# Score products over the 48 rows that hold parts, without zero fills, in a decoder layer with two attentions and experts

## The chip, the cores and the metric

The kernel runs on one core of one Trainium2 chip. The metric is the device time of one execution, in microseconds (us), as the median of the timed runs. One execution was taken by the profiler.

## What is computed

Input are x and a context, 16 batches of 128 tokens by 128 features in fp32. Both attentions have 16 heads of 8 features. Cut to what matters:

```
q, k, v = heads(x @ Wq.T + bq), heads(x @ Wk.T + bk), heads(x @ Wv.T + bv)
eq, ek  = heads(x @ Weq.T + beq), heads(x @ Wek.T + bek)
scores  = q k^T * SCALE
esc     = eq ek^T * SCALE * decay          # decay = exp(-0.1 |i - j|)
attn    = softmax(scores + 0.5 * esc)
ctx     = attn @ mixed(v)                  # v plus two gated, head-wise products
x = layernorm(x + layernorm(x + ctx @ Wo.T + bo) * ln_g + ln_b)
x = layernorm(x + cross_attention(x, context, context))   # plain softmax attention
x = layernorm(x + experts(x))              # 16 experts, top 4, silu(g) * u, all computed densely
```

## The kernel before

**Parts.** The score products are made in bf16 with the accuracy of fp32: each projected q and k is split into three bf16 parts (high, middle, lowest), and six products of parts are summed by one matmul. So a head's contraction has 6 parts x 8 features = 48 rows (`NP = 6`, `HD = 8`, `R = NP * HD`). The parts are written to DRAM (`spill`) and read back in the order of rows (`stack1`, `stack2`) into the buffers `stk[0]` and `stk[1]`: partitions 0 to 47 hold the parts, for q and k, all heads and, in the first attention, both kinds (plain and entangled). Partitions 48 to 127 are filled with zeros once at the start, and every score matmul contracts over all 128 partitions:

```
dst = stk[b.par][:].rearrange("p a h u t -> p a h (u t)")
sp.dma_start(dst[0:R, :, at:at + H // 2], src[:, :, at:at + H // 2]
```

`stk2` is the same memory, cut in four for the second attention. Later the expert layer uses `stk` as scratch.

**Stages.** Set-up (weights transposed, first parts), first attention, second attention, expert layer. In the attentions every engine runs a program written out by hand: a slot is one step over the batches, a unit (0 to 3 in a slot) is a group of four heads, and each operation works on the batch of its own lag. Engines are tied by semaphores alone, and each works strictly in its program's order. Loops over slots are hardware loops with the same body.

**TensorE in the first attention, unit by unit** (line numbers as in the profile; four matmuls each unless said):
- every unit: entangled scores L699 (`entangled_score`); then what the unit has of its own; scores L709 (`score`); then the rest of its own; then the maximum of the unit before is subtracted by a matmul, L717 (one, 512 columns), and the probabilities of two units before are transposed, L727.
- of its own: unit 0 the output product L816 between L699 and L709; unit 1 the weighted sum L789 (16 matmuls over 32 columns of weights) between them and the transposes L803 at the end; unit 2 projections L677 between them and behind L709; unit 3 L789 between them and L812 behind L709.

VectorE multiplies the entangled scores by the decay (L1463), adds and takes the maximum (L1475); ScalarE takes the exponent (L1143) and copies the transposed probabilities (L1169) and the sums `pvs` (L1178).

**TensorE in the second attention:** every unit: L738 (`score2`, scores into bank 0, of which VectorE's L1486 takes the maximum; the next L738 waits for it), L760 (`score_t`, the same scores transposed), L767 (the maxima are subtracted, four matmuls). Behind that: unit 1 L789 and L812; unit 2 L816 and then L751 (one transpose of the maxima, 16 columns of weights); unit 3 L789 and L803. Unit 0 begins with the projections L687 and L688. ScalarE's exponent is L1153.

**Zero fills.** VectorE's first instruction fills `stk[0]` (L1384), GpSimd fills `stk[1]` behind its loads of biases (L469), VectorE fills `top_t` (L1386). SyncE waits for the first two before the first `stack1` of each buffer.

Of the kernel before, what the change touches and what calls it, by code (L numbers as in the profile page):

```python
# [13 lines left out]
F32 = mybir.dt.float32  # L14
# [26 lines left out]
R = NP * HD  # L41
# [42 lines left out]
def head(g, j):  # L84

    return 2 * GH * (g // 2) + 2 * j + g % 2
# [8 lines left out]
def build(nc, a, k, out):  # L95
    with ExitStack() as ctx:  # L96
        def sb(name, shape, dt=F32):
            return ctx.enter_context(nc.sbuf_tensor(name, shape, dt))

        def sem(name):  # L100
            return ctx.enter_context(nc.semaphore(name))
# [52 lines left out]
        stk = [sb(f"stk{p}", [128, 2, H, 2, S], BF16) for p in range(2)]  # L154

        stk2 = [stk[k % 2][:].rearrange("p a h u t -> p a (h u t)")[:, :, k // 2 * H * S:k // 2 * H * S + H * S]
                .rearrange("p a (h t) -> p a h t", t=S) for k in range(4)]
# [12 lines left out]
        top_t = sb("top_t", [128, 2, S], BF16)  # L170
# [41 lines left out]
        bank = [ctx.enter_context(nc.psum_tensor(f"bank{i}", [128, 512], F32)) for i in range(8)]  # L212
# [58 lines left out]
                self.var_eps = sem(f"var_eps{n}")  # L271
                self.rstd = sem(f"rstd{n}")
        L1, L2 = Layer(1, slice(0, 2)), Layer(2, slice(0, 1))
        zeroed = [sem("zeroed0"), sem("zeroed1"), sem("zeroed2")]
        TAIL1, TAIL2 = 3, 5
        root = [sem("root0"), sem("root1")]
        root_step = [sem("root_step0"), sem("root_step1")]
# [42 lines left out]
        E_BANK = (2, 5)  # L320
# [4 lines left out]
        def _(sp):  # L325
# [23 lines left out]
            def spill(L, b):  # L349

                sp.wait_ge(L.low, b.n + 1)
                if L is L1:
                    src = by_part[b.par].rearrange("p k u t -> p k (u t)")
                    dst = scr1[bass.ds(b.n, 1)].rearrange("b a s p u t -> p (b a) s (u t)")
                else:
                    src = by_part[b.par][:, :, 0, :]
                    dst = scr2[bass.ds(b.n, 1)].rearrange("b a s p t -> p (b a) s t")
                for side in range(2):
                    sp.dma_start(dst[:, side, 0:3], src[:, 3 * side:3 * side + 3]).then_inc(L.spilled[b.par], 16)
                    sp.dma_start(dst[:, side, 3:5], src[:, 4 * side:4 * side + 2]).then_inc(L.spilled[b.par], 16)  # L360
                sp.dma_start(dst[:, :, 5], src[:, HIGH]).then_inc(L.spilled[b.par], 16)

            def stack1(b, half):

                if half == 0:
                    sp.wait_ge(L1.spilled[b.par], b.pair * L1.spill_step + L1.spill_step)
                if not isinstance(b.n, int) or b.n >= 2:
                    sp.wait_ge(L1.scores, NG * b.n - NG - NM + NM * half)
                src = scr1[bass.ds(b.n, 1)].rearrange("b a s (f h) u t -> (b s f) a h (u t)", h=H)
                dst = stk[b.par][:].rearrange("p a h u t -> p a h (u t)")  # L370
                at = H // 2 * half
                sp.dma_start(dst[0:R, :, at:at + H // 2], src[:, :, at:at + H // 2]
                             ).then_inc(L1.stacked[2 * b.par + half], 16)
# [12 lines left out]
            def pair1(p):  # L386
                for par in range(2):
                    b = Batch(p, par)
                    if isinstance(p, int) and p == 0:
                        sp.wait_ge(zeroed[par], 1)  # L390
                    stack1(b, 0)
                    if b.back(-1).live:
                        spill(L1, b.back(-1))
                    stack1(b, 1)

            spill(L1, Batch(0, 0))
            pair1(0)
            load_ffn()
            with sp.Fori(1, NB // 2 - 1) as p:
                pair1(p)  # L400
            pair1(NB // 2 - 1)

            def quad2(q):
# [47 lines left out]
        def _(pool):  # L451
            def rows(dst, src):
                n = src.shape[0]
                pool.dma_start(dst, src.unsqueeze(0).broadcast_to([128, n])).then_inc(in_rows, 16)
# [11 lines left out]
            rows(ln_b[:], a["L0_attn_ln_b"])  # L466
            rows(bv2[:], a["L0_xattn_bv"])
            rows(bo2[:], a["L0_xattn_bo"])
            pool.memset(stk[1][:].rearrange("p a h u t -> p (a h u t)").bitcast(F32), 0.0).then_inc(zeroed[1], 1)  # L469
            pool.memset(minus_half[:], -0.5)  # L470
            pool.memset(eps_col[:], EPS)
            pool.memset(zero_col[:], 0.0)
# [194 lines left out]
        def _(pe):  # L667
# [23 lines left out]
            def entangled_score(b, g):  # L691

                u = b.n * NG + g
                if g in (0, 2):
                    pe.wait_ge(L1.stacked[2 * b.par + g // 2], b.pair * 16 + 16)
                if not isinstance(u, int) or u >= 2:
                    pe.wait_ge(L1.picked, u - 1)
                for j in range(GH):
                    m = pe.matmul(bank[E_BANK[g % 2]][:, 128 * j:128 * j + 128], stk[b.par][:, 0, head(g, j), 1, :],  # L699
                                  stk[b.par][:, 1, head(g, j), 1, :], start=True, stop=True)  # L700
                m.then_inc(L1.ent_scores, 1)

            def score(b, g):

                u = b.n * NG + g
                if not isinstance(u, int) or u >= 2:
                    pe.wait_ge(L1.exped, u - 1)
                for j in range(GH):
                    m = pe.matmul(bank[g % 2][:, 128 * j:128 * j + 128], stk[b.par][:, 0, head(g, j), 0, :],  # L709
                                  stk[b.par][:, 1, head(g, j), 0, :], start=(j == 0), stop=True,  # L710
                                  skip_group_check=True)
                m.then_inc(L1.scores, 1)

# [16 lines left out]
            def score2(b, g):  # L730

                u = b.n * NG + g
                if g == 0:
                    pe.wait_ge(L2.stacked[b.buf], b.quad * L2.stack_step + L2.stack_step)
                if not isinstance(u, int) or u >= 1:
                    pe.wait_ge(L2.maxed, u)
                for j in range(GH):
                    m = pe.matmul(bank[0][:, 128 * j:128 * j + 128], stk2[b.buf][:, 0, head(g, j), :],  # L738
                                  stk2[b.buf][:, 1, head(g, j), :], start=True, stop=True)
                m.then_inc(L2.scores, 1)  # L740

            def turn_top(b):
# [11 lines left out]
            def score_t(b, g):  # L754

                u = b.n * NG + g
                if not isinstance(u, int) or u >= 2:
                    pe.wait_ge(L2.exped, u - 1)
                for j in range(GH):
                    pe.matmul(bank[2 + g % 2][:, 128 * j:128 * j + 128], stk2[b.buf][:, 1, head(g, j), :],  # L760
                              stk2[b.buf][:, 0, head(g, j), :], start=(j == 0), stop=True,
                              skip_group_check=True)
                if g == 0:
                    pe.wait_ge(L2.top_t_ev, b.n + 1)
                for j in range(GH):
                    h = GH * g + j
                    m = pe.matmul(bank[2 + g % 2][:, 128 * j:128 * j + 128],  # L767
                                  neg_ident[:, h:h + 1].broadcast_to([128, 128]), top_t[:, b.par, :],
                                  start=False, stop=True, skip_group_check=True)
                m.then_inc(L2.shifted, 1)  # L770
# [108 lines left out]
            for i, w in enumerate((WQ, WEQ, WK, WEK)):  # L879
                t = pe.transpose(bank[0][:, 128 * i:128 * i + 128], wn[:, w, :], ident[:])  # L880
# [20 lines left out]
            for i, w in enumerate((WV, WO, XQ, XK)):  # L901
                t = pe.transpose(bank[1][:, 128 * i:128 * i + 128], wn[:, w, :], ident[:])
# [20 lines left out]
            for b in range(NB):  # L923
                if b >= 4:
                    pe.wait_ge(dve_set, DV_WALL + b - 3)
                pe.matmul(bank[b % 4][:, 0:VSZ], x_t[:, 128 * b:128 * b + 128], wall[:],
                          start=True, stop=True).then_inc(pe_set, 1)
# [4 lines left out]
            for c in range(4):  # L932
                pe.wait_ge(act_set, c + 2)
                for j in range(4):
                    t = pe.transpose(bank[C_BANK[c]][:, 128 * j:128 * j + 128], c_tok[:, 4 * c + j, :], ident[:])
# [165 lines left out]
        def _(act):  # L1101
# [54 lines left out]
            def take_top(b):  # L1156
                act.wait_ge(L2.top_t, b.n + 1)
                if isinstance(b.n, int) and b.n == 0:
                    act.wait_ge(zeroed[2], 1)
                if not isinstance(b.n, int) or b.n >= 2:  # L1160
                    act.wait_ge(L2.shifted, NG * b.n - NG)
                act.copy(top_t[0:H, b.par, :], bank[6][0:H, 256:256 + S // 2].bitcast(BF16)).then_inc(L2.top_t_ev, 1)
# [206 lines left out]
        def _(dve):  # L1369
            made = [0]  # L1370

            def step(ins):
                made[0] += 1
                ins.then_inc(dve_set, 1)
                return made[0]
# [5 lines left out]

                dve.memset(waiter[:, n:n + 1], 0.0)

            dve.memset(stk[0][:].rearrange("p a h u t -> p (a h u t)").bitcast(F32), 0.0).then_inc(zeroed[0], 1)  # L1384
            step(dve.memset(half_pi[:], math.pi / 2))
            dve.memset(top_t[:].rearrange("p a t -> p (a t)").bitcast(F32), 0.0).then_inc(zeroed[2], 1)  # L1386

            dve.wait_ge(in_bias, 7 * 16)
            n = step(dve.tensor_copy(bias_perm[:].rearrange("r (f h) -> r f h", h=H),
# [412 lines left out]
```

## Time and profile before

| | us |
|---|---|
| timed runs, median (lowest to highest) | 391.68 (390.48 to 393.94) |
| the profiled execution | 396.48 |
| its span, first to last instruction | 394.7 |
| busy: TensorE matmuls | 341.8 (87%) |
| busy: TensorE weight loads | 263.2 (67%) |
| busy: VectorE | 271.2 (69%) |
| busy: ScalarE | 224.1 (57%) |
| busy: GpSimd | 217.6 (55%) |
| mean granted TensorE clock | 0.959 of full |

The engines are called PE (TensorE's matmuls), PEld (its weight loads), DVE (VectorE), ACT (ScalarE), POOL (GpSimd) and SP (SyncE) in the rows. The ends of matmuls are modelled, so their busy times overlap; starts are what was recorded. "128*32" is the shape of the stationary operand, rows by columns. Idle time is given with what ended it: "issue" means that nothing which the profile shows held the instruction up.

### The profile page before, as it was taken

The page shows a single profiled execution, that of the slowest core. Times are in us where ns is not written, and L with a number is a line of the kernel's source. Part 1 is how long each engine was busy: PE and PEld are TensorE (multiplying, and loading weights), DVE is VectorE, ACT ScalarE, POOL GpSimd, SP SyncE. Part 2 cuts the span into 40 slices and gives each one's busy share as a digit, 9 for nine tenths or more (in the row PEclk, how much of TensorE's full clock was granted, in tenths as well). Part 3 has the DMA queues.
Part 4 walks back from the last instruction along what each step waited for, and adds up shares of the span by engine and source line. Part 5 has one row for each costly group of instructions (what it writes and reads, how often), then busy time and mean ns, then how long its engine had stood idle before and what let it go on. Part 6 is the DMA issues. An engine that isn't in the chain of part 4 may idle for free. (4 is left out here: it accounts for less than half of the span.)

```text
span 394.7 us, 11535 instructions
## 1 busy us (share of the span) xinstructions
PE 341.8 (87%) x3556; PEld 263.2 (67%) x3556; DVE 271.2 (69%) x1247; ACT 224.1 (57%) x527; POOL 217.6 (55%) x405
## 2 busy tenths in 40 slices
PE   2885899999999997986789899998796999999992
PEld 1764778777887776774678777777563756566662
DVE  5643999999999997965446667666953149644453
ACT  1546487899989985685566667664461341222220
POOL 8777345788888984885743333320114244655551
PEclk9989599999999999998799999999999899999997
DMA  6989898789899887246344655671006420443410
GB/s 120 233 226 202 164 219 199 163 208 201 201 181 197 190 189 171 54 91 150 84 98 111 149 131 141 129 149 28 2 22 195 139 75 7 96 151 102 139 28 27
DMA packets 76927, 52.89 MB, mean 134 GB/s; under 512 B 34448, under 2 KB 68064, under 8 KB 76880
## 3 DMA queue, kind: packets, MB, share of 16 engines
q1 hardware_dynamic: 75840, 51.73, 56.0%
q0 software_dynamic: 512, 0.48, 0.9%
q8 instruction: 24, 0.39, 0.5%
q14 instruction: 23, 0.19, 0.2%
q10 hardware_dynamic: 528, 0.10, 0.2%
HBM read 32.24 MB, written 20.05 MB: 132 GB/s over the span
## 5 line engine op out<-in xcount | busy, mean ns | idle before, releaser
L1475 DVE CUSTOM_DVE_ANT_0 bank<-bank,decayed_e 128x128 f32<-128x128 f32 x256 | 67.2, 325 | 1.1 <-issue 0.5
L1486 DVE TENSOR_REDUCE top<-bank 128x4 bf16<-128x512 f32 x64 | 44.2, 690 | 29.5 <-PE bank L738 29.1
L646 POOL TENSOR_TENSOR stk<-stk 128x512 f32<-128x512 f32 x32 | 40.7, 1276 | 40.8 <-ACT stk L1349 39.3
L1153 ACT ACTIVATE prob_t<-bank 128x512 f32<-128x512 f32 x64 | 38.1, 597 | 34.0 <-PE bank L767 33.5
L1721 DVE TENSOR_TENSOR stk<-bank,stk 128x512 f32<-128x512 f32 x32 | 22.1, 692 | 46.1 <-POOL stk L646 45.0
L1349 ACT ACTIVATE stk<-bank 128x512 f32<-128x512 f32 x32 | 19.0, 597 | 54.5 <-PE bank L1049 53.0
L481 POOL TENSOR_TENSOR rest<-pf,parts 128x512 f32<-128x512 f32 (+1 forms) x32 | 29.2, 914 | 37.3 <-ACT parts L1132 37.1
L1143 ACT ACTIVATE prob<-bank 128x512 f32<-128x512 f32 x64 | 39.3, 613 | 17.4 <-PE bank L717 16.8
L789 PE MATMUL bank<-prob_t,vmix 128*32 128x128 f32 x1024 | 43.0, 281 | 5.9 <-ACT pvs L1178 5.9
L487 POOL TENSOR_TENSOR parts<-rest,parts 128x512 bf16<-128x512 f32 (+1 forms) x32 | 29.2, 914 | 30.1 <-ACT parts L1136 30.0
L1062 PEld LDWEIGHTS bank<-w,stk 128*128 128x128 f32 x256 | 33.4, 193 | 17.1 <-issue 8.6
L1463 DVE TENSOR_TENSOR decayed_e<-bank,decay 128x512 f32<-128x512 f32 x64 | 44.0, 688 | 0.3 <-issue 0.3
L727 PE MATMUL bank<-ident,prob 128*128 128x128 f32 x256 | 39.8, 279 | 0.0
L1169 ACT COPY prob_t<-bank 128x512 f32<-128x512 f32 x64 | 38.4, 600 | 1.0 <-PE bank L727 1.0
L1475 DVE DVE_READ_ACCUMULATOR2_ANT shift<- 128x1 bf16 x256 | 37.1, 145 | 0.0
L738 PE MATMUL bank<-stk 128*128 128x128 bf16 x256 | 26.2, 227 | 12.0 <-DVE top L1486 10.8
L727 PEld LDWEIGHTS bank<-ident,prob 128*128 128x128 f32 x256 | 31.0, 143 | 6.7 <-issue 2.5
L1062 PE MATMUL bank<-w,stk 128*128 128x128 f32 x256 | 34.3, 278 | 0.9 <-DVE stk L1721 0.9
L789 PEld LDWEIGHTS bank<-prob_t,vmix 128*32 128x32 f32 x1024 | 26.0, 110 | 13.2 <-issue 7.9
L1053 PE MATMUL bank<-x_t,w 128*128 128x512 f32 x64 | 33.6, 607 | 0.0
L1049 PE MATMUL bank<-x_t,w 128*128 128x512 f32 x64 | 33.5, 606 | 0.0
L738 PEld LDWEIGHTS bank<-stk 128*128 128x128 bf16 x256 | 17.7, 103 | 18.5 <-DVE top L1486 11.4
(201 smaller groups left out, 804.8 us busy)
## 6 DMA issues: line engine op xcount, KB each, us to landing
stk<-parts_dram SPq DMA_DIRECT2D x32, 384.0 KB, 5.5
stk<-shares_dram SPq DMA_DIRECT2D x64, 128.0 KB, 3.0
parts_dram<-parts SPq DMA_DIRECT2D x32, 192.0 KB, 2.4
parts_dram<-parts SPq DMA_DIRECT2D x48, 128.0 KB, 2.4
stk<-parts_dram SPq DMA_DIRECT2D x32, 192.0 KB, 3.7
parts_dram<-parts SPq DMA_DIRECT2D x32, 96.0 KB, 2.0
parts_dram<-parts SPq DMA_DIRECT2D x48, 64.0 KB, 1.8
w<-in_L_ffn_w_dram SPq DMA_DIRECT2D x3, 512.0 KB, 9.2
```

The lines of the kernel that those rows point to most:

```text
L646: pool.tensor_tensor(h1[kk % 2], sg[kk % 2], share[kk], ALU.mult).then_inc(weighted, 1)
L727: t = pe.transpose(bank[3][:, 128 * j:128 * j + 128], prob[g % 2][:, j, :], ident[:])
L738: m = pe.matmul(bank[0][:, 128 * j:128 * j + 128], stk2[b.buf][:, 0, head(g, j), :], stk2[b.buf][:, 1, head(g, j), :], start=True, stop=True)
L789: w = pe.matmul(bank[at][32 * j:32 * j + 32, 128 * m:128 * m + 128], vmix[b.par][:, head(2 * m, j) // 2, e:e + 2, :].rearrange("p e f -> p ...
L1053: pe.matmul(bank[UP_BANK[u % 3]][:], w3[:, 128 * kk:128 * kk + 128], xt, start=True, stop=True).then_inc(up_mm, 1)
L1062: m = pe.matmul(bank[4 + c % 2][:, 128 * t:128 * t + 128], actt[u % 3][:, 128 * t:128 * t + 128], w2[:, kk, :], start=(kk == 0 and t == 0) ...
L1143: act.activation(prob[g % 2][:].rearrange("p h t -> p (h t)"), bank[g % 2][:], ACT.Exp).then_inc(L.exped, 1)
L1153: act.activation(prob_t[g][:].rearrange("p h t -> p (h t)"), bank[2 + g % 2][:], ACT.Exp).then_inc(L2.exped, 1)
L1169: act.copy(prob_t[g][:].rearrange("p h t -> p (h t)"), bank[3][:]).then_inc(L.turned_ev, 1)
L1463: dve.tensor_tensor(decayed_e[:, g % 2], bank[E_BANK[g % 2]][:].rearrange("p (h t) -> p h t", h=GH), decay[:].unsqueeze(1).broadcast_to([1 ...
L1475: m = dve.tensor_tensor_reduce(out=bank[g % 2][:, 128 * j:128 * j + 128], in0=bank[g % 2][:, 128 * j:128 * j + 128], in1=decayed_e[:, g % ...
L1486: dve.tensor_reduce(top[:, b.par, GH * g:GH * g + GH], bank[0][:].rearrange("p (h t) -> p h t", h=GH), AX.X, ALU.max).then_inc(L2.maxed, 1)
```

## The change

All score matmuls of both attentions (L699, L709, L738, L760) take partitions 0 to 47 of both operands instead of all 128. The two fills of `stk` go, and with them SyncE's waits. The fill of `top_t` stays. No other instruction is added, removed or moved on any engine.

```diff
-        zeroed = [sem("zeroed0"), sem("zeroed1"), sem("zeroed2")]
+        zeroed = sem("zeroed")
...
-                    if isinstance(p, int) and p == 0:
-                        sp.wait_ge(zeroed[par], 1)
                     stack1(b, 0)
...
-            pool.memset(stk[1][:].rearrange("p a h u t -> p (a h u t)").bitcast(F32), 0.0).then_inc(zeroed[1], 1)
...
-                    m = pe.matmul(bank[E_BANK[g % 2]][:, 128 * j:128 * j + 128], stk[b.par][:, 0, head(g, j), 1, :],
-                                  stk[b.par][:, 1, head(g, j), 1, :], start=True, stop=True)
+                    m = pe.matmul(bank[E_BANK[g % 2]][:, 128 * j:128 * j + 128], stk[b.par][0:R, 0, head(g, j), 1, :],
+                                  stk[b.par][0:R, 1, head(g, j), 1, :], start=True, stop=True)
...
-                    m = pe.matmul(bank[g % 2][:, 128 * j:128 * j + 128], stk[b.par][:, 0, head(g, j), 0, :],
-                                  stk[b.par][:, 1, head(g, j), 0, :], start=(j == 0), stop=True,
+                    m = pe.matmul(bank[g % 2][:, 128 * j:128 * j + 128], stk[b.par][0:R, 0, head(g, j), 0, :],
+                                  stk[b.par][0:R, 1, head(g, j), 0, :], start=(j == 0), stop=True,
                                   skip_group_check=True)
...
-                    m = pe.matmul(bank[0][:, 128 * j:128 * j + 128], stk2[b.buf][:, 0, head(g, j), :],
-                                  stk2[b.buf][:, 1, head(g, j), :], start=True, stop=True)
+                    m = pe.matmul(bank[0][:, 128 * j:128 * j + 128], stk2[b.buf][0:R, 0, head(g, j), :],
+                                  stk2[b.buf][0:R, 1, head(g, j), :], start=True, stop=True)
...
-                    pe.matmul(bank[2 + g % 2][:, 128 * j:128 * j + 128], stk2[b.buf][:, 1, head(g, j), :],
-                              stk2[b.buf][:, 0, head(g, j), :], start=(j == 0), stop=True,
+                    pe.matmul(bank[2 + g % 2][:, 128 * j:128 * j + 128], stk2[b.buf][0:R, 1, head(g, j), :],
+                              stk2[b.buf][0:R, 0, head(g, j), :], start=(j == 0), stop=True,
                               skip_group_check=True)
...
-            dve.memset(stk[0][:].rearrange("p a h u t -> p (a h u t)").bitcast(F32), 0.0).then_inc(zeroed[0], 1)
             step(dve.memset(half_pi[:], math.pi / 2))
```

## Rows read from the trace of the kernel before

**Rows 1.** Busy time by stretch: us, PE, PEld, DVE, ACT, POOL, clock, DMA, GB/s.

```profile
37.90:175.30 137.40, 125.63 (x1519) 105.09 (x1520) 126.92 (x833) 111.00 (x266) 100.73 (x237) 0.96 0.81 175
175.30:292.00 116.70, 102.17 (x1509) 82.39 (x1507) 75.38 (x234) 70.93 (x183) 42.34 (x95) 0.96 0.45 100
```

**Rows 2.** Timeline, PE, first attention: start, us, operation, idle before in brackets.

```profile
99.46 0.38 PE L803 MATMUL bank<-ident,pvs 128*128 128x128 f32 x2
...
101.34 0.60 PE L727 MATMUL bank<-ident,prob 128*128 128x128 f32 x4
101.77 0.39 PE L699 MATMUL bank<-stk 128*128 128x128 bf16 x4
102.09 0.67 PE L789 MATMUL bank<-prob_t,vmix 128*32 128x128 f32 x16
102.69 0.40 PE L709 MATMUL bank<-stk 128*128 128x128 bf16 x4
102.92 0.28 PE L812 MATMUL bank<-ident,attn_o 128*128 128x128 f32 x1
103.04 0.38 PE L717 MATMUL bank<-shift,neg_ident 128*128 128x512 bf16 x1
...
103.69 0.39 PE L699 MATMUL bank<-stk 128*128 128x128 bf16 x4
103.91 0.44 PE L816 MATMUL bank<-wo_t,attn_ot 128*128 128x128 f32 x2
104.26 0.40 PE L709 MATMUL bank<-stk 128*128 128x128 bf16 x4
...
105.29 0.39 PE L699 MATMUL bank<-stk 128*128 128x128 bf16 x4
106.13 0.67 PE L789 MATMUL bank<-prob_t,vmix 128*32 128x128 f32 x16 [0.46 <-ACT pvs L1178]
...
107.62 0.38 PE L803 MATMUL bank<-ident,pvs 128*128 128x128 f32 x2
```

**Rows 3.** Timeline, PEld, first attention, behind the weighted sum.

```profile
102.68 0.23 PEld L709 LDWEIGHTS bank<-stk 128*128 128x128 bf16 x4 [0.20 <-issue]
```

**Rows 4.** Timeline, PE and PEld, set-up: the transposes of the last weights.

```profile
12.73 0.64 PE L905 MATMUL bank<-ident,wn 128*128 128x128 f32 x2
13.30 0.34 PE L906 MATMUL bank<-ident,gates_n 48*128 48x48 f32 x1
...
12.95 0.42 PE L905 MATMUL bank<-ident,wn 128*128 128x128 f32 x1
...
13.30 0.18 PEld L906 LDWEIGHTS bank<-ident,gates_n 48*128 48x128 f32 x1 [0.33 <-issue]
```

**Rows 5.** Timeline, PE, second attention.

```profile
226.05 0.39 PE L738 MATMUL bank<-stk 128*128 128x128 bf16 x4
...
226.72 0.44 PE L816 MATMUL bank<-xw_t,attn_ot 128*128 128x128 f32 x2
227.09 0.22 PE L751 MATMUL bank<-ident_bf,top 128*16 128x128 bf16 x1
227.25 0.40 PE L738 MATMUL bank<-stk 128*128 128x128 bf16 x4
...
229.78 0.39 PE L767 MATMUL bank<-top_t,neg_ident 128*128 128x128 bf16 x4
230.51 0.40 PE L738 MATMUL bank<-stk 128*128 128x128 bf16 x4 [0.34 <-DVE top L1486]
```

**Rows 6.** A stretch at half clock: its busy times (columns as in rows 1), and PE's timeline.

```profile
195.20:197.50 2.30, 2.30 (x24) 1.69 (x22) 0.23 (x1) 0.89 (x2) 0.94 (x2) 0.50 0.03 5
...
195.49 1.10 PE L789 MATMUL bank<-prob_t,vmix 128*32 128x128 f32 x16
196.52 0.80 PE L687 MATMUL bank<-x_t,xw_t 128*128 128x128 f32 x2
```

**Rows 7.** Timeline of the set-up: DVE, POOL and PE around the second zero fill.

```profile
9.41 4.62 DVE L1412 TENSOR_SCALAR bv_cols<-bv_cols,bias_t 128x128 f32<-128x128 f32 x1
9.61 4.49 DVE L1414 TENSOR_SCALAR neg_ident<-ident 128x128 bf16<-128x128 f32 x1
...
9.75 3.53 POOL L469 MEMSET stk<- 128x4096 f32 x1
...
15.46 1.53 PE L889 MATMUL bank<-ident,x_tok 128*128 128x128 f32 x12 [0.26 <-DMA x_tok<-in_x_dram]
```

More of the change, by code:

```diff
@@ L1158, in take_top @@
                 if isinstance(b.n, int) and b.n == 0:
-                    act.wait_ge(zeroed[2], 1)
+                    act.wait_ge(zeroed, 1)
                 if not isinstance(b.n, int) or b.n >= 2:
@@ L1382, in carry @@
                 dve.memset(waiter[:, n:n + 1], 0.0)
-            dve.memset(stk[0][:].rearrange("p a h u t -> p (a h u t)").bitcast(F32), 0.0).then_inc(zeroed[0], 1)
             step(dve.memset(half_pi[:], math.pi / 2))
-            dve.memset(top_t[:].rearrange("p a t -> p (a t)").bitcast(F32), 0.0).then_inc(zeroed[2], 1)
+            dve.memset(top_t[:].rearrange("p a t -> p (a t)").bitcast(F32), 0.0).then_inc(zeroed, 1)
             dve.wait_ge(in_bias, 7 * 16)
```

## The prediction

> **What bounds the kernel now.** I read the busy times by stage first [rows 1]. They split the 394.7 us span into a set-up, the stretch of the first attention (37.9 to 175.3 us), that of the second (175.3 to 292.0 us) and the expert layer behind it. The diff edits two things: 1024 of TensorE's matmuls with their weight loads (four groups of 256: 16 batches by 16 heads), which all lie in the two middle stretches, and two zero fills in the set-up. In the first attention VectorE is busy for 126.92 of 137.40 us and TensorE for 125.63: both are nearly full, and neither has much to give. In the second VectorE has 75.38 of 116.70 and TensorE 102.17, so there TensorE sets the pace.
>
> Busy time does not say how much room TensorE has, since the ends of its matmuls are modelled and overlap. Starts do. So next I read TensorE's timeline over one slot (one batch) of the first attention [rows 2]. A slot lasts 107.62 - 99.46 = 8.16 us, from one L803 to the next. Four 128-column bf16 matmuls take 0.22 to 0.23 us from their start to the next group's start (102.69 to 102.92, 103.69 to 103.91), that is 0.055 us each. The only idle time printed in that slot is 0.46 us before the weighted sum L789 of unit 1. Measured by starts it is 106.13 - 105.29 = 0.84 us, where the same pair in unit 3 takes 102.09 - 101.77 = 0.32: 0.52 us of slack a slot. That is all the room TensorE has there.
>
> **Narrower contraction, the matmuls themselves.** A matmul streams its moving columns, 128 before and after, and the stationary operand keeps 128 columns. None of the spacings above contains the number of rows. Nearest row: L906 contracts over 48 rows, its load takes 0.18 us and its matmul 0.34 against 0.42 for the 128-row transposes L905 [rows 4]; but it also streams only 48 columns, 80 fewer, which at the 1.2 GHz level is 0.067 us of the 0.08. So the shape itself is worth between nothing and 0.02 us a matmul in latency, and nothing in spacing. I take nothing.
>
> **Narrower contraction, its neighbours.** This is the term that counts. Today all score matmuls have the shape of what stands around them, 128 rows by 128 columns, and the load of the next stationary operand is drawn ahead of the running matmuls. Where the shape changes, the trace shows that it isn't:
> - Into the weighted sum (128*32): the last of four bf16 matmuls starts at 101.77 + 0.165 = 101.94, and L789 at 102.09: 0.155 us where 0.055 is usual. A change costs 0.10 us [rows 2].
> - Out of it, TensorE's weight loads stand still for 0.20 us, and the releaser is "issue", so no semaphore holds them [rows 3].
> - Out of the 128*16 transpose L751 into the scores: 227.25 - 227.09 = 0.16 us, again 0.10 more than 0.055. Into it, behind fp32: the second L816 starts 0.165 us after 226.72, so L751 comes 0.20 us later, where fp32 neighbours follow each other in 0.11 (four L727 and the next group: 101.77 - 101.34 = 0.43). (The second L816 is 0.44 less one such matmul's 0.28 behind the first.) Again 0.09 to 0.10 [rows 2, 5].
> - Is a change of rows alone enough? One instruction tells: L906 stands behind two L905 with no wait between, loads 48*128 instead of 128*128, and its load stood idle for 0.33 us "issue". The second L905 starts at 12.95 and L906 at 13.30: 0.35 us, where the two L905 lie 0.22 apart [rows 4]. At the same matmul length (0.42, the level at which 195.49 stands) the exit from the 128*32 shape takes 196.52 - (195.49 + 1.10 - 0.42) = 0.35 us [rows 6]. The row change costs just what the column change costs there. This row decides my forecast.
>
> The Trainium skill, page "TensorEngine Tiling (Array Packing)", section "Key Properties", has a rule for this: changing the tiling mode drains TensorE, and its list of modes has row tiles of 64 for a contraction up to 64. The trace agrees, with its 0.35 us before L906 [rows 4]; the rule says nothing of the price. By the rule with that price the sum is the one below, by a chip without it the sum would be nothing.
>
> So I count shape changes by the order of the program, unit by unit. First attention, before: into and out of L789 in units 1 and 3, so 4 a slot. After: the entangled scores (48) stand between a transpose L727 (128) and what follows, and the scores L709 (48) between that and L717 (128). Unit 0: into and out of L699, into and out of L709, with L816 between them: 4. Unit 2 the same with the projection: 4. Units 1 and 3: into L699, L699 to L789, L789 to L709, out of L709: 4, two of them there already. That is 16 against 4: 12 new ones a slot, 12 x 0.10 = 1.20 us. Of it the 0.52 us before L789 can take its share, because ScalarE's copy of the sums, for which L789 waits, doesn't depend on where TensorE lost its time within the unit. Left: 0.68 us a slot, x 16 = 10.9 us. VectorE, today the fuller engine, then waits for TensorE.
>
> Second attention, before: into and out of L789 twice, and into and out of L751: 6. After: L738 and L760 stand together, so a unit has one entry and one exit. Exits L760 to L767: 4 new. Entries: behind L812 (unit 2), behind L688 (unit 0) and behind L767 (unit 1) are new, that of unit 3 behind L751 exists. 7 new a slot. Of these one exit and one entry fall into the place where L738 waits for VectorE's maximum: from 229.78 to 230.51, 0.73 us, of which 0.22 are L767's own and 0.51 slack [rows 5]. Left: 5 x 0.10 = 0.50 us, x 16 = 8.0 us.
>
> Each new change is a hole of a tenth of a microsecond on TensorE; behind it in its queue stand the max subtraction L717 or the shift L767, for which ScalarE's exponentials wait.
>
> **Zero fills.** VectorE's fill stood first on its engine, before it waited for a bias transfer. GpSimd's took 3.53 us at 9.75. While it ran, two of VectorE's short TENSOR_SCALARs took 4.62 and 4.49 us, ending at 14.03 and 14.10 [rows 7]: GpSimd and VectorE hold each other up there. Without it VectorE's chain behind them comes up to 1.1 us earlier. But TensorE then sits until 15.46 for the transfer of x (releaser DMA) whatever VectorE does [rows 7], and the projections behind it wait for ScalarE, which waits for TensorE. Gain: between 0 and 1.1 us; I take 0, as the transfer is the row on the path. SyncE's two waits on these fills are met long before they are reached: nothing. The third fill (top_t) stays.
>
> **The sum.** 10.9 + 8.0 + 0 = 18.9 us. On the profiled execution's own 396.48 us that gives 415.4. This execution was 4.8 us above the median of the timed runs (391.68), and I have nothing in the sum that depends on this difference, so I put the term on the median: 410.6, rounded 410.5.
>
> Bounds. The low end is 0.07 us a change: L906's extra was 0.35 - 0.22 = 0.13 at the slow level, and if all of it scales with the clock, half remains. Then (12 x 0.07 - 0.52) x 16 = 5.1 and 5 x 0.07 x 16 = 5.6: 10.7, less 1.1 for the fills: 401.3. The high end has nothing absorbed: (12 + 7) x 0.10 x 16 = 30.4: 422. It would come if the loop from scores to maximum to shift to exponent and back to the same bank, two units long, is lengthened by each hole in it, so that slack and loss don't meet. The timed runs themselves lie 3.5 us apart (390.48 to 393.94), so I put the low end at 398.
>
> **Rivals.**
> Not slower, the other side: the row count changes nothing in how loads are drawn ahead. Place: the loads of L699, L709, L738 and L760. It decides at a price per change of 0.04 us, below which the slack takes all of the first attention (12 x 0.04 = 0.48) and the second keeps 5 x 0.04 x 16 = 3.2 us, within one per cent. For it: only one 48-row load stands in the trace; against it: that one waited, without a semaphore. It gives 391.7 less 0 to 1.1 us for the fills: 391. The Trainium skill, page "TensorE: Matmul & The Clock Gate", section "LDWEIGHTS (loading the stationary operand)", says that a 32x128 load takes as long as a 128x128 one and that only columns matter. That rule alone leads to this rival; no row here contradicts it for the length of a load, but it says nothing of what stands before the load.
>
> Faster: fewer rows deliver a result sooner. Place: the second attention's loop on bank 0, scores, maximum, next scores, which runs at 227.25 - 226.05 = 1.20 us. At the 0.02 us above, on 4 units x 16 it gives 1.3 us, with the fills 2.4: 389. It would need no drain at all as well.
>
> More than forecast: the thinner stream lets TensorE's granted clock fall. Where it is at half (195.2 to 197.5, shown as 0.50 [rows 6]), 16 L789 and the exit take 1.03 us instead of 0.60. If a tenth of the two middle stretches (254 us) ran so, 18 us come on top: 429. Against it: the holes are 0.1 us, and today's longer ones of 0.5 us a slot leave the stretches at 0.96.
>
> **How the numbers follow.** Forecast 0.80, no drain 0.11, faster 0.05, clock 0.04. The range is the forecast's own, 398 to 422, with 0.20 outside. One per cent (3.9 us) is about what a measurement of this kernel can tell from no change. Slower by over that: 0.80 and the clock's 0.04 make 0.84. Within it: the no-drain case and part of the faster one, 0.13. Faster: 0.03.
>
> **What would show it.** Right: the weight loads of the four groups show idle time put down to issue at nearly every entry; the slot of the first attention grows from 8.16 to about 8.8 us, the 0.46 us wait of L789 is gone, and VectorE's L1463 and L1475 wait for TensorE; the second attention's slot gains about 0.5 us; matmul and load lengths stay at 0.22 and 0.10. The TENSOR_SCALARs at 9.4 us become short, and the first scores still start near 37.9 us. Wrong: starts still 0.055 us apart across the new borders, which would be the first rival; or slots longer with borders unchanged, which would be a cause I haven't seen.

## The result, and the profile after

The changed kernel takes 430.56 us (428.98 to 431.22) against 392.81 (390.48 to 394.99) of the kernel before: 9.6% more, ratio 1.0956, 95% interval 1.0878 to 1.1034. It is slower, as forecast, but by 37.8 us and not by 18.9; 430.6 lies outside the range of 398 to 422. The profiled execution took 431.22 us, its span is 429.4 us, and its mean granted clock 0.885 where that of before was 0.959. Single executions that lie far above the others of their kernel are named where they occurred, and the ratios leave them out.

First the two slots, where the granted clock was full. TensorE's timeline in the first attention, to be held against [rows 2] (L724 was L727, L696 was L699, L786 was L789, L706 was L709, L714 was L717, L813 was L816, L800 was L803):

```profile
97.96 0.38 PE L800 MATMUL bank<-ident,pvs 128*128 128x128 f32 x2
...
102.27 0.38 PE L714 MATMUL bank<-shift,neg_ident 128*128 128x512 bf16 x1
102.48 0.60 PE L724 MATMUL bank<-ident,prob 128*128 128x128 f32 x4
103.02 0.40 PE L696 MATMUL bank<-stk 48*128 48x128 bf16 x4
103.34 0.49 PE L813 MATMUL bank<-wo_t,attn_ot 128*128 128x128 f32 x2
103.76 0.39 PE L706 MATMUL bank<-stk 48*128 48x128 bf16 x4
104.09 0.39 PE L714 MATMUL bank<-shift,neg_ident 128*128 128x512 bf16 x1
...
104.85 0.40 PE L696 MATMUL bank<-stk 48*128 48x128 bf16 x4
105.20 0.67 PE L786 MATMUL bank<-prob_t,vmix 128*32 128x128 f32 x16
...
106.80 0.38 PE L800 MATMUL bank<-ident,pvs 128*128 128x128 f32 x2
```

The slot takes 106.80 - 97.96 = 8.84 us instead of 8.16. Into the 48-row scores: L724 to L696 takes 103.02 - 102.48 = 0.54 us where [rows 2] has 0.43. Out of them: L706 to L714 0.33 instead of 0.23, L696 to L813 0.32 instead of 0.22. The 0.46 us wait before the weighted sum is gone: L786 follows L696 after 0.35. The weight loads show the same from their side. In the timeline of PEld, each load of the entangled scores (four a slot) stands idle for 0.17 us, released by nothing but issue. Before the loads of the scores L706 an idle time is printed only behind the weighted sum; where they stand behind L813, as in the second line, none is, and the hole shows in the starts alone:

```profile
103.01 0.22 PEld L696 LDWEIGHTS bank<-stk 48*128 48x128 bf16 x4 [0.17 <-issue]
...
103.76 0.22 PEld L706 LDWEIGHTS bank<-stk 48*128 48x128 bf16 x4
...
104.84 0.22 PEld L696 LDWEIGHTS bank<-stk 48*128 48x128 bf16 x4 [0.17 <-issue]
```

In the second attention, TensorE's timeline, the answer to [rows 5] (L735 was L738, L757 was L760, L764 was L767):

```profile
231.07 0.39 PE L735 MATMUL bank<-stk 48*128 48x128 bf16 x4
231.31 0.38 PE L757 MATMUL bank<-stk 48*128 48x128 bf16 x4
231.62 0.40 PE L764 MATMUL bank<-top_t,neg_ident 128*128 128x128 bf16 x4
...
233.85 0.44 PE L800 MATMUL bank<-ident,pvs 128*128 128x128 f32 x2
...
235.22 0.40 PE L764 MATMUL bank<-top_t,neg_ident 128*128 128x128 bf16 x4
235.85 0.40 PE L735 MATMUL bank<-stk 48*128 48x128 bf16 x4 [0.23 <-DVE top L1482]
...
240.37 0.44 PE L800 MATMUL bank<-ident,pvs 128*128 128x128 f32 x2
```

L757 to L764 takes 0.31 us (four bf16 matmuls without a border: 0.22). The slot, L800 to L800, takes 6.52 us. Of the kernel before, the same row (L803) four slots apart is

```profile
228.62 0.44 PE L803 MATMUL bank<-ident,pvs 128*128 128x128 f32 x2
...
252.72 0.44 PE L803 MATMUL bank<-ident,pvs 128*128 128x128 f32 x2
```

so 24.10 / 4 = 6.03 us. The two slots account for (8.84 - 8.16) x 16 + (6.52 - 6.03) x 16 = 10.9 + 7.8 = 18.7 us, the sum of the forecast. The other 19 us aren't there at full clock. They show in the granted clock. Of the changed kernel, here are the page's line of 40 slices, busy times by stretch with the granted clock in the third column from the end, and the transposes L724 at the end of the first low stretch, at half and at full clock:

```profile
PEclk9987555999999999999558999999655999999998
...
38.98:195.00 156.02, 152.68 (x1518) 110.21 (x1518) 131.36 (x832) 112.88 (x265) 100.85 (x236) 0.89 0.71 154
195.00:324.00 129.00, 123.01 (x1465) 89.67 (x1465) 74.19 (x227) 70.33 (x182) 42.00 (x94) 0.83 0.41 90
...
55.77:70.22 14.45, 14.45 (x96) 9.91 (x95) 7.31 (x44) 7.11 (x16) 4.46 (x8) 0.50 0.56 121
97.96:106.80 8.84, 8.84 (x100) 6.36 (x99) 8.07 (x54) 7.65 (x19) 7.03 (x18) 1.00 0.79 178
...
73.34 1.06 PE L724 MATMUL bank<-ident,prob 128*128 128x128 f32 x4
...
75.97 0.60 PE L724 MATMUL bank<-ident,prob 128*128 128x128 f32 x4
```

and the same of the kernel before (its transposes are L727):

```profile
PEclk9989599999999999998799999999999899999997
...
38.50:46.00 7.50, 6.03 (x36) 4.92 (x35) 7.27 (x40) 2.46 (x4) 2.92 (x6) 0.50 1.25 225
...
46.91 1.06 PE L727 MATMUL bank<-ident,prob 128*128 128x128 f32 x4
...
48.78 0.60 PE L727 MATMUL bank<-ident,prob 128*128 128x128 f32 x4
```

[rows 1] had 0.96 in both attentions; now it is 0.89 and 0.83. Both kernels fall to half (1.2 GHz) at 37 to 38 us, behind a wait of 3.2 us for ScalarE's copy. The kernel before is back at 2.4 GHz at about 48 us, the changed one only at about 74 us, and it falls twice more, for 24 us (from 204) and 31 us (from 303). In its low stretch TensorE is not idle: a whole slot there, 55.77 to 70.22, shows it busy for all of 14.45 us. The slot costs 14.45 instead of 8.84 us. As the clock is either full or half, the time at half clock in all is 2 x (1 - 0.885) x 429.4 = 99 us, against 2 x (1 - 0.959) x 394.7 = 32. So 66 us more at half clock go with the 19 us, 0.29 us each; a full slot loses 1 - 8.84 / 14.45 = 0.39 of its low time.

The set-up: VectorE's TENSOR_SCALARs that took 4.62 and 4.49 us [rows 7] are short now, and nothing comes of it: TensorE's projections behind them start at 13.69 us, where they started at 13.57.

```profile
9.54 0.29 DVE L1408 TENSOR_SCALAR bv_cols<-bv_cols,bias_t 128x128 f32<-128x128 f32 x1
9.74 0.86 DVE L1410 TENSOR_SCALAR neg_ident<-ident 128x128 bf16<-128x128 f32 x1
...
38.98 0.58 PE L696 MATMUL bank<-stk 48*128 48x128 bf16 x4 [0.72 <-issue]
```

The first scores start at 38.98 us, a microsecond later than before (37.93). Most of it is TensorE with half-clock lengths for longer: the eight projections from 13.69 take 2.07 us instead of 1.52, the last four transposes before the scores 1.12 instead of 0.66.

### The profile page after: what moved, and what is told of

Read it like the earlier page. It is cut to its first block, busy times and chain, and to the rows that moved or that the text cites. A ratio compares the mean times of both kernels' runs of the same rounds, so it can differ in the third digit from the quotient of the medians.

```text
span 429.4 us, 11531 instructions
## 1 busy us (share of the span) xinstructions
PE 395.5 (92%) x3556; PEld 280.1 (65%) x3556; DVE 269.1 (63%) x1246; ACT 226.9 (53%) x527; POOL 214.4 (50%) x404
## 4 chain that ended last, share of the span: by engine, by line
PE 57%; POOL 15%; issue 13%; DVE 8%; ACT 3%; DMA 1%; POOLq 1%; SPq 1%; DVEq 0%; ACTq 0%
PE bank L786 7%; PE bank L735 6%; PE bank L764 5%; PE bank L757 4%; PE bank L1046 3%; PE bank L674 3%; PE bank L724 3%; PE bank L1050 3%; PE bank L1059 3%; DVE top L1482 2%; POOL parts L484 2%; POOL rstd L525 2%; PE bank L923 2%; PE bank L696 2%; PE bank L714 2%
## 5 line engine op out<-in xcount | busy, mean ns | idle before, releaser
L1459 DVE TENSOR_TENSOR decayed_e<-bank,decay 128x512 f32<-128x512 f32 x64 | 43.9, 687 | 8.7 <-issue 7.5
L786 PE MATMUL bank<-prob_t,vmix 128*32 128x128 f32 x1024 | 48.3, 307 | 0.6 <-ACT pvs L1175 0.6
L724 PE MATMUL bank<-ident,prob 128*128 128x128 f32 x256 | 42.7, 294 | 0.0
L724 PEld LDWEIGHTS bank<-ident,prob 128*128 128x128 f32 x256 | 35.0, 152 | 6.3 <-issue 2.1
L786 PEld LDWEIGHTS bank<-prob_t,vmix 128*32 128x32 f32 x1024 | 29.0, 119 | 8.7 <-issue 3.4
L735 PE MATMUL bank<-stk 48*128 48x128 bf16 x256 | 28.2, 238 | 4.3 <-DVE top L1482 4.3
L764 PE MATMUL bank<-top_t,neg_ident 128*128 128x128 bf16 x256 | 29.3, 246 | 0.0
```

The lines of the kernel that those rows point to most:

```text
L724: t = pe.transpose(bank[3][:, 128 * j:128 * j + 128], prob[g % 2][:, j, :], ident[:])
L764: m = pe.matmul(bank[2 + g % 2][:, 128 * j:128 * j + 128], neg_ident[:, h:h + 1].broadcast_to([128, 128]), top_t[:, b.par, :], start=False ...
L786: w = pe.matmul(bank[at][32 * j:32 * j + 32, 128 * m:128 * m + 128], vmix[b.par][:, head(2 * m, j) // 2, e:e + 2, :].rearrange("p e f -> p ...
L1459: dve.tensor_tensor(decayed_e[:, g % 2], bank[E_BANK[g % 2]][:].rearrange("p (h t) -> p h t", h=GH), decay[:].unsqueeze(1).broadcast_to([1 ...
```

## The experiments

All were made from the kernel before (fills kept) unless it says otherwise. A border is a place in TensorE's order where the shape changes, as between 128-row and 48-row matmuls. The theories: **border**, each border costs 0.10 us; **thin**, the 48-row scores themselves keep the granted clock low for longer; **holes**, the gaps at the borders do that.

**1. How many rows make a border.** The four score products, at 96 and at 64 rows:

```diff
-                    m = pe.matmul(bank[g % 2][:, 128 * j:128 * j + 128], stk[b.par][:, 0, head(g, j), 0, :],
-                                  stk[b.par][:, 1, head(g, j), 0, :], start=(j == 0), stop=True,
+                    m = pe.matmul(bank[g % 2][:, 128 * j:128 * j + 128], stk[b.par][0:96, 0, head(g, j), 0, :],
+                                  stk[b.par][0:96, 1, head(g, j), 0, :], start=(j == 0), stop=True,
...
```

The other three are altered alike; at 64 rows it is `0:64`.

> Scores contract over 96 rows, of which 48 to 95 are zeros; fills kept. Theory 'border': only a contraction of up to 64 rows is another shape for TensorE, so loads are drawn ahead as before: no idle 'issue' before L699 and L738, 390 to 396 us, slot of the first attention 8.16 us, clock 0.96. Rival 'thin': fewer active rows alone keep the clock down; then the borders are cheap but the low-clock stretch behind 38 us is longer than the 8 us of before, 396 to 412 us. Rival 'any count': every count but 128 is a border: about 430 us.

> Scores contract over 64 rows, 48 to 63 zeros; fills kept. Border: the same as the changed kernel, 427 to 433 us, slot 8.85 us at full clock. Thin: a little less than the changed kernel, as there are more rows at work, 420 to 430 us. Both: the fills play no part.

Measured at 96 rows: 394.86 us against 394.34, ratio 1.0033 (0.9983 to 1.0082). No border, no loss. The timeline of its weight loads shows the scores' load right behind its neighbours, with no idle time:

```profile
97.97 0.36 PEld L727 LDWEIGHTS bank<-ident,prob 128*128 128x128 f32 x3
98.29 0.32 PEld L699 LDWEIGHTS bank<-stk 96*128 96x128 bf16 x4
98.57 0.30 PEld L816 LDWEIGHTS bank<-wo_t,attn_ot 128*128 128x128 f32 x2
```

So it isn't "any count but 128". At 64 rows the borders are there (a slot of 8.85 us) and the time is 416.71 us (412.12 to 425.43), not the 427 to 433 expected if only the borders counted. The thin theory's direction was right, but the time lies 3 us below its range too.

**2. One attention at a time.** `[0:48]` in L699 and L709 alone, or in L738 and L760 alone.

> 48 rows in the first attention alone; fills kept. Border, 0.7 us a slot at full clock is 11 us; the low-clock stretch from 38 to 77 us adds 10 to 14: 413 to 419 us, second attention as before (slot 6.0 us). If the clock were a matter of that run alone and not of the change: 403 us.

> 48 rows in the second attention alone; fills kept. Border: 0.5 us a slot is 8 us, and a longer low-clock stretch at its start adds 3 to 8: 403 to 409 us; first attention as before (slot 8.16 us). first48 and second48 together should make up the whole 37.8 us; if they make clearly less, the two stretches share a cause.

First attention alone: 411.56 us, ratio 1.0485 (1.0406 to 1.0565), a little below the range expected. Its slot at full clock is 8.84 us, and the clock comes back at about 58 us. Second alone: 417.43 us, ratio 1.0642 (1.0554 to 1.0730), more than expected: its mean clock is 0.892 to 0.912, though the border's share there is the smaller one. Together 17.2 + 23.1 = 40.3 us, against 37.8 for both: each stretch pays for itself.

**3. The fills.** 48 rows in both attentions, both fills and their waits kept.

> 48 rows in both attentions as in the changed kernel, but with both zero fills and their waits. If the fills play no part: 427 to 433 us, low clock from 38 to about 77 us as there. If the moment at which the scores start decides how long the clock stays low (the 64-row kernel, which kept the fills, was out of it at 45 us): 412 to 420 us.

433.63 us (430.23 to 438.14), ratio 1.0986 (1.0870 to 1.1102). The interval holds the changed kernel's 1.0956: no part of the loss can be put down to the fills.

**4. Borders at full rows.** Six small matmuls a slot, of 48 rows or of 128, ahead of L699 in each unit and ahead of L709 in units 0 and 2, all scores at 128 rows:

```diff
+            def tick(to):
+                pe.matmul(to[:, 0:16], ident_bf[0:48, :], neg_ident[0:48, 0:16], start=True, stop=True,
+                          skip_group_check=True)
...
+                tick(bank[E_BANK[g % 2]])
...
+                if g in (0, 2):
+                    tick(bank[g % 2])
```

> The kernel before (scores over 128 rows) with six small matmuls a slot of 48 rows and 16 columns in the first attention, each overwritten by the scores behind it: 12 new borders a slot as in the change, at full rows. Border: the first attention's slot goes from 8.16 to about 9.1 us (12 x 0.10 plus 6 short matmuls, less the slack), 406 to 415 us, low-clock stretch at least as long as before. Thin rows as the cause: within 398 us.

> The same six small matmuls over 128 rows, so no border: the price of the added instructions alone. Both: 391 to 397 us, slot 8.16 to 8.25 us, as 6 x 0.055 fits in the slack of 0.52.

48-row ticks: 401.34 us, ratio 1.0156 (1.0102 to 1.0210), below the border's range and above the thin one's. The same ticks at 128 rows: 395.37 us, ratio 1.0011 (0.9978 to 1.0044). The timeline of the first:

```profile
101.22 0.60 PE L734 MATMUL bank<-ident,prob 128*128 128x128 f32 x4
101.75 0.18 PE L692 MATMUL bank<-neg_ident,ident_bf 48*128 48x16 bf16 x1
101.87 0.40 PE L704 MATMUL bank<-stk 128*128 128x128 bf16 x4
...
103.68 0.38 PE L810 MATMUL bank<-ident,pvs 128*128 128x128 f32 x2
```

101.75 - 101.22 = 0.53 us into the tick where 0.43 is usual, and 0.12 out of it where the 128-row tick has 0.03. The slot is 8.72 us (the next L810 comes at 112.40), 0.51 above that of the 128-row ticks (8.21). So twelve borders, less the slack, cost about what they cost in the changed kernel (0.68), without one thin score. What this kernel does not have is the long low stretch: its slices are

```profile
PEclk9988899999999999899999999999999899999997
```

and the mean clock of its four runs is 0.968 to 0.976, above that of before (0.950 to 0.964 in the runs beside it). I had expected its low stretch to be at least as long as before, and it is not: among 128-row scores, holes on TensorE don't keep the clock low (tried in the first attention only). So it takes the thin scores. That it takes them alone is not shown, since below 96 rows every thin score here brought borders with it; experiments 7 and 8 vary the one with the other held.

**5. Is it the state at the start?** The changed kernel, with 66 bf16 matmuls into an unused bank during TensorE's waits from 33 to 38 us; and the same in the kernel before.

```diff
+            def keep_warm(n):
+                for _ in range(n):
+                    pe.matmul(bank[0][:, 0:128], ident_bf[:], neg_ident[:], start=True, stop=True)
...
+                if c == 3:
+                    pe.wait_ge(dve_set, DV_WALL + NB - 3)
+                    keep_warm(56)
                 pe.wait_ge(act_set, c + 2)
...
+            keep_warm(10)
             pe.wait_ge(act_set, 8)
```

> The changed kernel plus 66 bf16 matmuls of 128 columns into an unused bank while TensorE waits for the last context copy and for the first scores (33 to 38 us), so that the clock is full when the scores begin. Theory 'border plus late clock': the long low stretch of 38 to 77 us goes, 413 to 420 us, slots 8.85 and 6.5 us. Rival 'thin stream keeps the clock down whatever it was': it falls again soon after 38 us and the time stays at 426 to 432.

> The kernel before plus the 66 matmuls that fill TensorE's waits from 33 to 38 us. Its low-clock stretch at 38 to 47 us costs about 4 us. If the fill keeps the clock up: 388 to 391 us. If it only moves the fall to some microseconds later, as with 48 rows (low from 44 to 57 us there): 392 to 396 us.

Changed kernel: 427.97 us (426.10, 426.51, 429.43 and one of 445.98), ratio 1.0838 (1.0748 to 1.0927). Without that one it is 4 us less than the changed kernel, with overlapping intervals. The first scores now run at full clock, and then it falls all the same:

```profile
39.78 0.39 PE L696 MATMUL bank<-stk 48*128 48x128 bf16 x4 [0.25 <-ACT c_t L1262]
...
42.21 0.39 PE L714 MATMUL bank<-shift,neg_ident 128*128 128x512 bf16 x1 [1.37 <-DVE shift L1479]
...
43.50 0.55 PE L706 MATMUL bank<-stk 48*128 48x128 bf16 x4
43.98 1.22 PE L674 MATMUL bank<-x_t,wqk 128*128 128x128 f32 x4
```

Four projection matmuls take 1.22 us from 43.98 on, at 42.86 they took 0.71. Behind the pipeline's fill with its waits of more than 1 us it is low until about 60 us: the transposes L724 take 1.06 us at 59.52 and 0.60 at 62.04. So the rival named in the expectation held, in the fall and in the time: a clock that is full at the start doesn't spare the scores the low stretch. It was 17 us long instead of 37, and little of that is seen in the median, as the clock also fell in the second attention. Kernel before with the same: 393.09 us, ratio 0.9986 (0.9945 to 1.0026), no difference; there too the fall only moved, to 44 us.

**6. Fewer rows still.** The four products over rows 0 to 31. Two of the six products of parts are left out of every score.

> Scores contract over rows 0 to 31 alone, so two of the six products of parts are left out; fills kept. The borders are as many as with 48 or 64 rows. If only the borders counted, and 48 rows against 64 (433.6 against 416.7 us) were chance: 412 to 434 us, not to be told from those. If fewer rows at work keep the clock low for longer: more than the 433.6 us of 48 rows, 436 to 450 us, mean clock below 0.87, and slots at full clock still 8.85 and 6.5 us.

430.99 us, ratio 1.0958 (1.0867 to 1.1050), mean clock 0.880 to 0.884, beside one run of 449.44 us at 0.836. It is the 48-row time, not more: the expectation from the thin theory that each step down costs more is refuted.

**7. The same scores with fewer borders.** The changed kernel with L816's product and both projections behind L709, so that L699 and L709 stand together in units 0 and 2; and the same order at 128 rows.

```diff
-                if g == 0 and b4.live:
-                    out_product(L1, b4, wo_t[:])
-                if g == 2 and ahead.live:
-                    project1(ahead, 0)
                 if b.live:
                     score(b, g)
+                if g == 0 and b4.live:
+                    out_product(L1, b4, wo_t[:])
                 if g == 2 and ahead.live:
+                    project1(ahead, 0)
                     project1(ahead, 1)
```

> The changed kernel with the first attention's order altered: the output product (unit 0) and the projections (unit 2) come behind the scores, so that entangled scores and scores stand together and share an entry and an exit. 12 borders a slot instead of 16. Border: slot at full clock 8.85 less 4 x 0.10 = 8.45 us, 6 us less in all, 421 to 427 us. If the slot is bound by something else (VectorE's 8.1 us or the loop through the exponent): above 8.6 us and 426 to 433.

> The same altered order at 128 rows with fills, the control for the order alone: there are no borders to share, so 391 to 397 us and a slot of 8.16 us; slower if projections behind the scores delay the subtraction of the maximum, by 0.1 to 0.3 us a slot, up to 399.

At 48 rows: 417.41 us, ratio 1.0627 (1.0556 to 1.0697), 13 us less than the changed kernel and better than expected. The slot is 8.6 us (L800 at 102.58, 111.20, 119.75), 0.25 less instead of 0.40. The control says why: at 128 rows the order itself costs, 397.6 us, ratio 1.0111 (1.0029 to 1.0194), slot 8.3 to 8.4. (Its runs are 395.61, 397.14 and 398.06 us, and one of 1096.54 that nothing here explains.) So a good 0.4 for four borders, less the price of the order. The slots make 0.24 x 16 = 4 us of the 13; the rest is clock: 0.906 to 0.917, where the changed kernel had 0.883 to 0.890 and the 32-row kernel, run beside this one, 0.880 to 0.884. Its slices show the first low stretch as short as before the change, and the second attention, whose order is as it was, still with long ones:

```profile
PEclk9987799999999999995679999999559699999998
```

The control has 0.951 to 0.967, so the order itself doesn't raise the clock. At the same 48 rows the number of borders weighs in the clock too: thin scores and holes do it together.

**8. 64 against 48 rows, more full-row work, and half the scores.** First the two row counts side by side, five rounds.

> 64 rows with fills once more, five rounds. If the row count weighs in the clock: 412 to 422 us, mean clock 0.91 to 0.95, clearly under rows48_again. If the first 416.7 us was a matter of that day: 426 to 436.

> 48 rows with fills once more, five rounds: 428 to 436 us, mean clock 0.87 to 0.89, whichever theory; only the distance to 64 rows counts.

64 rows: 419.09 us (411.4 to 420.48), clock 0.916 to 0.948. Its lowest run, with the highest clock, lies where the borders alone would put it: 392.8 + 18.7 = 411.5. 48 rows: 432.65 us (430.07 to 436.49), clock 0.869 to 0.884, ratio to before 1.0993 (1.0931 to 1.1056). No run of one overlaps with one of the other, in time or in clock. The slots at full clock are alike (L803 at 104.04 and 112.89 with 64 rows, 107.43 and 116.27 with 48: 8.85 and 8.84 us). So the 13.6 us between them are clock, at the same borders. The rows added hold only zeros. The slices of both:

```profile
PEclk9987799999999999997799999999959999999997
```

```profile
PEclk9997589999999999995555799999557899999998
```

Then the changed kernel with four 128-row matmuls ahead of every L724:

```diff
+                for _ in range(4):
+                    pe.matmul(bank[3][:, 0:128], ident_bf[:], neg_ident[:], start=True, stop=True,
+                              skip_group_check=True)
                 for j in range(GH):
                     t = pe.transpose(bank[3][:, 128 * j:128 * j + 128], prob[g % 2][:, j, :], ident[:])
```

> The changed kernel plus four bf16 matmuls of 128 rows and 128 columns ahead of every four L724 (no new border): 0.22 us a unit, 0.88 a slot, 14 us at full clock if nothing hides them. If too little work at full rows keeps the clock low: the low stretch behind 38 us ends before 60 us, and the first attention's loss is made good, 423 to 433 us in spite of 14 us more work. If the holes alone keep it low: the stretch stays, 440 to 450 us.

435.8 us (431.24 to 435.84, and one of 447.75), ratio 1.1010 (1.0924 to 1.1097), between both expectations. Its slot holds 0.22 us more a unit, 14 us in all, yet the kernel is only 5 us above the changed one, with a clock of 0.899 to 0.918 (0.871 in the run of 447.75) and a first low stretch that ends at about 59 us. It speaks for too little work at full rows, but weakly: the 48-row kernel of the pair above, without the added work, ended its first low stretch at about 57 us.

Last, the entangled scores alone at 48 rows.

> Only the entangled scores of the first attention at 48 rows, fills kept. New borders a slot: two each in units 0 and 2, one each in 1 and 3: 6. Border: 0.60 us, of which the slack of 0.52 takes nearly all: slot 8.16 to 8.4 us, 392 to 397 us at the clock of before. With a longer low stretch from half of the scores being thin: up to 403 us.

399.21 us, ratio 1.0106 (1.0037 to 1.0176). Slot 8.42 us (L803 at 101.18 and 109.60), at the upper end: six borders of 0.10 less the slack would be 8.24. So the slack before L789 doesn't absorb all it could: a wait of 0.24 us for ScalarE's sums is left there. The clock is low for 10 us (36 to 46), as before (38 to 48).

## Why the prediction was right in kind and wrong in size

- **The row that decided, L906 in [rows 4], was read rightly.** A change of rows alone makes TensorE wait. It costs 0.10 us in and 0.10 out at full clock, as the column changes had shown. It is seen in the changed kernel, and the 48-row ticks made it without thin scores. The sign that VectorE then waits for TensorE shows weakly: it sat idle before L1459 (was L1463) for 8.7 us in all instead of 0.3, mostly put down to issue.
- **The count of borders and the slack: right in the sum.** 8.16 to 8.84 us and 6.03 to 6.52 us, forecast 8.84 (1.20 less 0.52) and 0.50 more. The 10.9 and 8.0 us are measured as 10.9 and 7.8. The entangled scores alone showed, however, that less of the slack is absorbed when the borders are few: 6 borders cost 0.26 us, where the forecast's way gives 0.08. A wait of 0.24 us stays before L789. That would fit a copy of ScalarE's that comes later when TensorE loses time ahead of it, against what the prediction says, but this was not tried. With all twelve borders the whole slack is gone, and the sum comes out even so.
- **The Trainium skill's rule** ("TensorEngine Tiling (Array Packing)", "Key Properties", a change of tiling mode drains TensorE) held: the runs show a hole of 0.10 us at each border. So did its list of modes as far as it was tried: 96 rows are as 128 (ratio 1.0033), while 64, 48 and 32 rows all have the borders (slots of 8.85, 8.84 and 8.84 us).
- **The step that failed is the clock.** The prediction put it as a rival with a chance of 0.04, "against it: the holes are 0.1 us, and today's longer ones of 0.5 us a slot leave the stretches at 0.96". It looked for the cause in the holes alone and found them too short. Among 128-row scores they are: the 48-row ticks leave the clock at 0.97. What it left out, and so put at nothing in the sum, is that the scores' own rows weigh: at 48 rows, in the same order with the same borders, the clock stays at half for longer than at 64 (0.869 to 0.884 against 0.916 to 0.948, 13.6 us). And among thin scores the holes weigh as well: four borders a slot fewer brought 0.906 to 0.917. Half of the loss, 19 of 37.8 us, is that lower clock. The rival's own number, 429 us, lies close to the measured 430.6, but by luck: it took a tenth of the two stretches, 25 us of work, at 0.72 us each, where the time at half clock grew by 66 us and cost 0.29 us each.
- **Zero fills: nothing, as forecast.** VectorE became free sooner, and TensorE started no sooner for it.
- **"Fewer rows deliver a result sooner"**: there is nothing of it. At 96 rows the time is that of 128, and the slots at 32, 48 and 64 rows are alike (6.51 us in the second attention).
- **The range** held no more than the borders' own bounds. With a rival of 18 us above it on record, at a chance set by an argument about holes alone, the range ended at 422 where the measured time is 430.6.

**What stays open.** By what the chip lets the clock fall or rise isn't shown. 48 and 32 rows give the same clock and 64 a better one, so it doesn't follow the number of rows alone; 96 rows are as good as 128, but they have no borders either. How long one low stretch lasts differs between executions: with 48 rows in both attentions the first one ended at 74, 73 and 57 us in three kernels that differ in the fills at most, while their mean clocks agree (0.885, 0.888, 0.884). Why the second attention pays more for its thin scores (15 of its 23 us are not borders) than the first (6 of 17) was not tried.

## What to carry to other kernels

A matmul over at most 64 rows between matmuls over 128 is a change of TensorE's shape, at 0.10 us for each entry and exit (32, 48 and 64 rows were tried). Filling the unused rows with zeros once and contracting over more than 64 (96 and 128 were tried) takes these borders away, and no run here shows a cost of the added rows. If narrow matmuls must be, put them side by side, and count borders in the program's order before anything else. Where a change makes matmuls thinner, look at the granted clock after each long wait of TensorE, and keep that as a case with a real chance: here it doubled the loss.

## What the runs showed of the hardware that I had not expected

- A TensorE whose records leave hardly any idle time can stay at half clock for 37 us (37 to 74 us, a slot of 14.45 us busy for 14.45), with 48-row scores among its work; at 128 rows the same program is back at full clock 10 us after the same fall (38 to 48 us).
- At the same 48 rows, four borders a slot fewer in the first attention raised the mean clock to between 0.906 and 0.917, from between 0.883 and 0.890.
- Rows that hold only zeros change the clock: 64 rows, of which 16 are zeros, ran 13.6 us faster than 48, by the clock alone.
- Sixteen-column ticks with a 48-row shape cost 6 us in the first attention (401.34 against 395.37 us) and left the mean clock higher than before (0.968 to 0.976 against 0.950 to 0.964 in the runs beside it).
- While GpSimd filled 16 KB a partition, a VectorE operation on 128 columns took 4.6 us; without that fill it took 0.29.
